# One row of products for both key blocks, and the transposes right behind it, in the two attentions of a hybrid layer stack

## The reference

```python
x = x + attn_a(layernorm(x))   # 16 heads of 16, unit-norm q and k, rotary on even heads, causal, softmax
x = x + ffn(layernorm(x))      # 64 experts, 4 per token, and a shared expert
x = x + attn_b(layernorm(x))   # 16 "heads" of 16, no mask, softmax, output projection with bias
x = x + ffn(layernorm(x))      # the same weights again

logits = einsum('bshd,bthd->bhst', q, k) * gain        # attn_a; attn_b: q k^T / sqrt(16)
attn   = softmax(where(causal, logits, -inf))
y      = einsum('bhst,bthd->bshd', attn, v) ; out = y @ w_out
```

## Time and profile before

| | us |
|---|---|
| three runs | 1283.98, 1289.21, 1290.45; median 1289.21 |
| the profiled execution | 1282.62 |
| its span, first to last instruction | 1279.6 |
| outside the span | 3.0 |

### The profile page before, as it was taken

The page is one execution under the profiler, slowest core; times in us unless marked ns, Lnnn a source line. Parts: engine busy times, 40 slices in busy tenths (PEclk is TensorE's granted clock), DMA queues, the critical chain, the costliest instruction groups (busy, mean ns, idle before and its releaser), DMA issues. The chain is left out here.

```text
span 1279.6 us, 23658 instructions
## 1 busy us (share of the span) xinstructions
PE 912.4 (71%) x7450; PEld 684.9 (54%) x7450; DVE 713.3 (56%) x2253; ACT 458.8 (36%) x973; POOL 496.6 (39%) x558
## 2 busy tenths in 40 slices
PE   3975999967178698993356699997727889799100
PEld 2753677656166576782244345556616667588100
DVE  3767888648155643454255689945805564345333
ACT  2542566621100244551143368861101024356000
POOL 3000322255445232325562344415544423232576
PEclk9986899979599898996677789997959889999655
DMA  6384899589812399863386466607411239986343
GB/s 220 70 153 74 167 231 231 199 193 239 209 66 88 116 276 270 248 206 103 83 181 152 80 94 109 91 1 188 121 70 66 78 120 277 264 255 208 111 135 115
DMA packets 159017, 197.06 MB, mean 154 GB/s; under 512 B 17328, under 2 KB 137648, under 8 KB 155824
## 3 DMA queue, kind: packets, MB, share of 16 engines
q1 hardware_dynamic: 104000, 97.70, 35.4%
q0 software_dynamic: 22848, 68.18, 16.8%
q10 hardware_dynamic: 32048, 29.70, 7.6%
HBM read 132.86 MB, written 90.18 MB: 174 GB/s over the span
## 5 line engine op out<-in xcount | busy, mean ns | idle before, releaser
L871 ACT ACTIVATE tmp<-ps 128x256 f32<-128x256 f32 (+1 forms) x328 | 146.1, 472 | 103.5 <-PE ps L824 33.9
L502 POOL DMA_INDIRECT xd<-big,slot x128 | 127.4, 995 | 128.3 <-DVE slot L1384 91.1
L969 ACT ACTIVATE tmp<-ps 128x384 f32<-128x384 f32 (+1 forms) x256 | 134.9, 544 | 63.6 <-PE ps L637 36.4
L541 POOL DMA_INDIRECT big<-yd,slot x128 | 125.9, 984 | 57.2 <-issue 32.0
L464 POOL COPY arena<-negmax 24x2048 bf16<-24x2048 bf16 x32 | 60.6, 1893 | 154.6 <-ACT negmax L871 126.7
L620 PE MATMUL ps<-arena 96*128 96x256 bf16 (+1 forms) x512 | 100.1, 283 | 13.8 <-DVEq L299 10.6
L634 PE MATMUL ps<-arena 120*128 120x256 bf16 (+1 forms) x512 | 101.9, 267 | 0.6 <-ACT tmp L969 0.2
L1008 ACT ACTIVATE tmp<-ps 128x512 f32<-128x512 f32 x32 | 19.0, 597 | 223.3 <-remote 110.9
L1106 DVE SCALAR_TENSOR_TENSOR X<-big,comb,X 128x256 f32<-128x256 f32 x128 | 58.5, 482 | 68.5 <-DMA big<-yd,slot 62.8
L1489 DVE SCALAR_TENSOR_TENSOR tmp<-tmp,ps 128x128 f32<-128x128 f32 x128 | 36.8, 288 | 99.0 <-ACT tmp L1037 98.6
L1428 DVE SCALAR_TENSOR_TENSOR tmp<-tmp,ps 128x512 f32<-128x512 f32 x32 | 21.9, 685 | 121.5 <-ACT tmp L1008 104.9
(11 more groups left out here) (178 smaller groups left out, 1913.1 us busy)
## 6 DMA issues: line engine op xcount, KB each, us to landing
big<-xd POOLq DMA_DIRECT2D x128, 256.0 KB, 4.8
arena<-parts SPq DMA_DIRECT2D x192, 128.0 KB, 6.0
xd<-zero SPq DMA_DIRECT2D x8, 2048.0 KB, 13.8
spill<-in_we SPq DMA_DIRECT2D x128, 128.0 KB, 2.8
yd<-tmp POOLq DMA_DIRECT2D x64, 256.0 KB, 3.1
yd<-tmp ACTq DMA_DIRECT2D x64, 256.0 KB, 3.6
parts<-arena SPq DMA_DIRECT2D x128, 96.0 KB
arena<-in_we SPq DMA_DIRECT2D x8, 1024.0 KB, 8.9
```

The lines of the kernel that those rows point to most:

```text
L502: pool.indirect_dma_start(xd[:, :], bass.IndirectOffsetOnAxis(ap=slot[:, i, k:k + 1], axis=0), xn_all[:, i, :], None).then_inc(scattered.s ...
L541: pool.indirect_dma_start(gring[n % GRING], None, yd[:, :], bass.IndirectOffsetOnAxis(ap=slot[:, b * TB + m % TB, m // TB:m // TB + 1], ax ...
L871: return act.activation(dst, src, ACT.Copy)
L969: act.activation(prob[h % 8][:, 0:n], ps[2 + h % 2][:, 0:n], ACT.Exp).then_inc(exp_ready.sem, 1)
```

## The change

`weigh` loses its argument `kb` and issues both key blocks of a group in one row, at the place where block 0 stood. `turn_group` of the group before follows it directly. So TensorE has at `h = 5`: `weigh` of group 0; at `h = 9` and `13`: `weigh` of group 1 or 2, then `turn_group` of group 0 or 1; at `h = 1` of the next step: `weigh` of group 3, `turn_group` of group 2; at `h = 5`: behind the new batch's `weigh`, `turn_group` of group 3. The other operations that depend on these move a head later on all three engines.

```diff
-                def weigh(b, g, kb):
-                    if kb == 0:
-                        if g == 0:
-                            pe.wait_ge(*vb_ready(r, b + 1))
-                        pe.wait_ge(*exp_ready(r, b * H + 4 * g + 4))
-                        pe.wait_ge(*ot_ready(r, b * 4 + g - 1))
-                    q0 = kb * P if causal(r) else 0
-                    for j in range(4):
-                        ...
-                    if kb == TB - 1:
-                        mm.then_inc(pv_done.sem, 1)
+                def weigh(b, g):
+                    if g == 0:
+                        pe.wait_ge(*vb_ready(r, b + 1))
+                    pe.wait_ge(*exp_ready(r, b * H + 4 * g + 4))
+                    pe.wait_ge(*ot_ready(r, b * 4 + g - 1))
+                    for kb in range(TB):
+                        q0 = kb * P if causal(r) else 0
+                        for j in range(4):
+                            ...
+                    mm.then_inc(pv_done.sem, 1)
...
-                        if third and h in (1, 2):
-                            weigh(s - 2, 3, h - 1)
-                        if second and h >= 5 and h % 4 in (1, 2):
-                            weigh(s - 1, (h - 5) // 4, h % 4 - 1)
+                        if third and h == 1:
+                            weigh(s - 2, 3)
+                            turn_group(s - 2, 2)
+                        if second and h in (5, 9, 13):
+                            weigh(s - 1, (h - 5) // 4)
+                            if h >= 9:
+                                turn_group(s - 1, (h - 9) // 4)
                         if second and h == 2:
                             turn_maxima(s - 1, 1)
-                        if third and h == 4:
+                        if third and h == 5:
                             turn_group(s - 2, 3)
-                        if third and h == 6 and r == 0:
+                        if third and h == 7 and r == 0:
                             turn_output(s - 2)
-                        if third and h == 7 and r == 0:
+                        if third and h == 8 and r == 0:
                             output(s - 2)
-                        if second and h in (8, 12, 16):
-                            turn_group(s - 1, h // 4 - 2)
...
-                        if third and h == 5 and r == 0:
+                        if third and h == 6 and r == 0:
                             take_turned(s - 2)
...
-                        if third and h == 0:
+                        if third and h == 1:
                             group(s - 2, 2)
-                        if third and h == 4:
+                        if third and h == 5:
                             group(s - 2, 3)
-                        if second and h in (8, 12):
+                        if second and h in (9, 13):
                             group(s - 1, h // 4 - 2)
-                        if third and h == 9 and r == 0:
+                        if third and h == 10 and r == 0:
                             dve.wait_ge(op_done.sem, s - 1)
                             add_out(s - 1, x_added, ps[7])
```

More of the change, by code:

```diff
@@ L638, in probs @@
                     mm.then_inc(s2_done.sem, 1)
-                def weigh(b, g, kb):
-                    if kb == 0:
-                        if g == 0:
-                            pe.wait_ge(*vb_ready(r, b + 1))
-                        pe.wait_ge(*exp_ready(r, b * H + 4 * g + 4))
-                        pe.wait_ge(*ot_ready(r, b * 4 + g - 1))
-                    q0 = kb * P if causal(r) else 0
-                    for j in range(4):
-                        h = 4 * g + j
-                        mm = pe.matmul(ps[4][32 * j:32 * j + VW, g % 2 * S + q0:g % 2 * S + S], vb[b % 3][:, kb, h, :],
-                                       prob[h % 8][:, kb * S:kb * S + S - q0], start=(kb == 0), stop=(kb == TB - 1))
-                    if kb == TB - 1:
-                        mm.then_inc(pv_done.sem, 1)
+                def weigh(b, g):
[6 more added lines that the diff above has]
+                        for j in range(4):
+                            h = 4 * g + j
+                            mm = pe.matmul(ps[4][32 * j:32 * j + VW, g % 2 * S + q0:g % 2 * S + S], vb[b % 3][:, kb, h, :],
+                                           prob[h % 8][:, kb * S:kb * S + S - q0], start=(kb == 0), stop=(kb == TB - 1))
+                    mm.then_inc(pv_done.sem, 1)
                 def turn_group(b, g):
```

## The result

| | before | changed |
|---|---|---|
| runs, us | 1276.41 to 1290.45, median 1285.42 (6) | 1295.02 to 1312.51, median 1303.17 (6) |
| span of the profiled execution | 1279.6 | 1297.7 |

The ratio is 1.0137, with a 95% interval of 1.0092 to 1.0182: slower by 12 to 23 us. The median that the prediction started from, 1289.21, is 3.8 above that of all six runs of the kernel before; so its 1304 lies close to the measured 1303.17, but the increase is 17.8 us for a forecast of 15. The number of instructions is the same.

What follows compares the result with a forecast made beforehand. TensorE seemed to bound both attentions; after the change ScalarE's loop would bind. Second attention +10.9 and first +4.8 took 1282.62 to 1298.3 us profiled, by the median 1289.2 + 15.7 = 1304.9, stated as 1304; range 1288 to 1313.

Steps and rivals of the forecast that it cites:

- What the merge saves: TensorE, both attentions: one row of both blocks 1.00 or 0.79 us; net 0.19 per group, 11.4 us of work.
- The loop through ScalarE: Second attention: exponential, copy, exponential, then TensorE's row, 3.79 us per four heads against 3.48; 1.24 per batch, 10.9 together.
- E11: Second attention, ScalarE: exponential of head 11, 0.60 us; its bank is reused by the probability product of head 13.
- E6 to C: Second attention, ScalarE: from the exponential of head 6 to the copy of a group, 0.60 us of the loop.
- C to E7: Second attention, ScalarE: from the copy of a group to the exponential of head 7, 0.30 us of the loop.
- The signs of being right: Second attention: rows 3.8 us apart, batch 15.1 to 15.2, TensorE idle about 0.5 before probability products of heads 9, 13, 1, 5.
- The transposes' move: TensorE: transposes behind the row take 0.27 us, 0.05 more than before, within 1.81 between probability products of heads 9 and 10.
- The wait of the maxima: First attention, h = 11: TensorE's maxima wait 0.93 us for VectorE's add, which moved a head later.
- The other groups of the first attention: Two groups per batch without output or maxima: loop 3.33 us against TensorE's 2.95; 0.2 each taken, batch +0.57.
- The closing stretches and the clock: First attention: step 8 costs 0.9 us, the end 0.5; clock stays. Rival: clock falls to 1.2 GHz, 1314 us, chance 0.05.
- TensorE as the bound: Rival, both attentions: TensorE bounds and its saving of 11.4 us shows, 1278 us; chance 0.10.
- VectorE's loop: Rival, second attention: VectorE takes over with its loop of some 6.9 us per eight heads, 1288 us; chance 0.08.

Runs made afterwards that it cites:

- The edit that takes it away: Changed kernel with VectorE's add moved ahead of group(0), to h = 9: first attention batch 15.93 us against 16.74, ratio to the kernel before 1.0093.
- the earlier copy: Changed kernel with ScalarE's copy of a group a head earlier: batches 16.62 and 13.94 us, ratio to the kernel before 1.0061.

## Why the prediction was right, step by step

- **What the merge saves.** Right. The row of both blocks is 1.07 long in the second and 0.86 in the first attention, with 1.00 from its start to the transposes (803.63 to 804.63), and these take 0.28 (0.27 predicted). The Trainium skill, "TensorEngine Tiling (Array Packing)", section "Key Properties", says that changing the tiling mode drains TensorE. The 1.00 for one row, where two rows took 0.57 each, agrees with that. The saving in products says nothing of the batch, which in the run of the merge alone is 14.02 for 13.92.
- **The loop through ScalarE.** Right as a mechanism, in the place named: ScalarE dry ahead of the first exponential behind each row, P13 held by E11 and so in every group. Shown twice, by the copy taken out of it (14.64 to 13.94) and by the exponentials shortened (13.76). The size was off: 3.66 per group where I had 3.79. The failing terms are E6 to C, 0.60, and C to E7, 0.30; in the changed kernel they are 0.50 and 0.26 (801.89, 802.39, 802.65). 3.79 - 0.14 = 3.65. I had taken both from a stretch where ScalarE waited for TensorE and not only for itself: the copy of the earlier trace rows starts at 847.93, right behind the end of the products that it copies (847.23 + 0.64 = 847.87, from the row of the kernel before under this list item), which in the changed kernel are long done by then. Per batch +0.72 instead of +1.24, and the second attention cost 7.3 us instead of 10.9. The signs of being right missed by as much: rows 3.66 apart and not 3.8, a batch of 14.64 and not 15.1 to 15.2, P13 late by 0.20 and not 0.5.

```profile
847.23 0.64 PE L649 MATMUL ps<-tmp 128*32 128x256 f32 x8
```

- **The transposes' move.** The 0.27 between P9 and P10 is rightly in the 1.81, but that the transposes had filled a wait before was missed, and with it which part of the change costs. By the prediction's own loop the moves alone would cost nothing (13.9) and the merge alone would gain (13.5); they came to 14.53 and 14.02, so the harm is nearly all in the moves.
- **The wait of the maxima.** Right: 1.03 measured for 0.93, with VectorE's order as described. The edit that takes it away gives back 0.81 per batch.
- **The other groups of the first attention.** The loop was put at 3.33, for two groups "without output or maxima". Only one is such, the one from h = 13, at 3.30; the one from h = 1 holds products of the maxima and is 3.42 for 3.28 before. Batch +0.76 for +0.57.
- **The closing stretches and the clock.** The first attention lost 8.2 and not 4.8. Six batches of 0.76 are 4.6, and 2.2 is the clock (below), on which the prediction said that it stays: a term that it had at nothing. What is left, 1.4, is what the prediction had for step 8 and the end (0.9 + 0.5). The last transposes wait as described: the two pairs at the end start 263.89 and 265.04, the second held by VectorE.
- **Rivals.** TensorE as the bound with 1278 us was wrong, and the run of the merge alone (1.0026) shows that it wouldn't have come without the moves either. VectorE's loop is real, at 6.88 per eight heads, and lies under the loop that decided (7.32).
- **Sum.** 1298.3 for the profiled execution, measured 1301.07 (its span is 1297.7). The attentions gave 15.5 of the 18.1 us of span, for 15.7 predicted. That they agree so well is luck: the first attention cost 3.4 more than predicted, most of it the clock, and the second 3.6 less. The remaining 2.6 come from stages that neither the change nor the prediction touches.

## What to carry to other kernels

An engine that is busy throughout a stretch need not be what a change of its work is measured by; ask first whether the others could follow when it gets faster. With two banks between two engines, ask for each stretch of two items what both must do in it, and place extra work where the other engine is behind anyway. Work that looks costly in the list may fill a wait and be all but free; here the transposes, moved, cost their full length, and the stretch that they left didn't shrink. The merge of small products paid here only once the engine fed in between had its own long item (the copy) in the gap that the longer row opens.

## What the hardware showed

The granted clock fell to 0.50 (1.2 GHz) at the end of the first attention. The rows are stretch, length, busy time of PE, PEld, DVE, ACT and POOL, granted clock, DMA share and GB/s, two of the changed kernel and then one of the kernel before:

```profile
263.00:268.00 5.00, 2.87 (x25) 1.66 (x25) 1.00 (x4) 1.03 (x3) 0.00 (x0) 0.74 0.00 0
268.00:272.00 4.00, 3.66 (x8) 2.40 (x8) 0.30 (x1) 0.00 (x0) 0.00 (x0) 0.50 0.00 0
258.00:262.00 4.00, 2.16 (x25) 1.07 (x23) 1.00 (x4) 1.13 (x3) 0.00 (x0) 1.00 0.00 0
```

TensorE there, in order of time, in the changed kernel and then in the kernel before:

```profile
266.08 1.11 PE L666 MATMUL ps<-ident,tmp 128*128 128x128 f32 x4 [0.62 <-DVE tmp L1228]
267.88 3.78 PE L675 MATMUL ps<-weights,tmp 128*128 128x256 f32 x8 [0.69 <-ACT tmp L871]
```

```profile
260.63 0.66 PE L667 MATMUL ps<-ident,tmp 128*128 128x128 f32 x4 [0.62 <-DVE tmp L1228]
261.97 1.99 PE L676 MATMUL ps<-weights,tmp 128*128 128x256 f32 x8 [0.69 <-ACT tmp L871]
```

So the clock was down before the four transposes, which took 1.11 for 0.66 (1.80 for 1.34 from their start to that of the projection); the last eight products of the projection took 3.78 for 1.99. Together that is 2.2 us. TensorE had stopped for 0.95, 0.72 and 0.62 us before them. The repeat on another chip has the same 3.78, and so has the kernel with short exponentials. It is 3.42 with the earlier copy and 1.99 in all the other kernels, also in the one with the add ahead of the group, which stops for the same 0.95 ahead of its last row of products. In the kernel before TensorE was busy 2.16 of 4.00 us and the clock stayed at 1.00. These traces don't say what decides.
